# Ten kinds of VectorE stages moved behind the next score maximum in a two-layer gated attention and expert kernel

## The chip, the cores and the metric

The kernel runs on one core of a Trainium2 chip. The time is that of one launch on the device in microseconds (µs), lower is better. Three runs of the kernel before took 998.27, 994.83 and 986.67 µs; the median is 994.83.

## The reference, cut to what matters

x is 8 batches of 256 rows of 256 numbers. Two layers follow one another, each a cross attention to a context and a feed-forward part, both added to x behind a tanh gate:

```
x = x + tanh(g_xattn[0]) * attention0(layernorm(x), ctx)   # 16 heads of 16, 256 context rows
x = x + tanh(g_ffn[0])   * experts0(layernorm(x))          # sigmoid router, best 4 of 8 experts in 2 of 4 groups,
                                                           # and a shared one: (silu(x Wg) * (x Wu)) Wd
x = x + tanh(g_xattn[1]) * attention1(layernorm(x), ctx)   # the same, scores clipped to +-10000, a NaN guard
x = x + tanh(g_ffn[1])   * experts1(x)                     # softmax router, best 2 of 8: relu(x W1 + b1) W2 + b2
```

Layer 0 computes all nine experts for every row and weighs them; layer 1 sends rows only to their two experts.

## The kernel before, in words

**Slots.** Attention is cut into 16 units (layer, batch) of 8 pairs of heads. One pair is one slot, so there are 128 slots; they are counted here from 0. A slot has two halves. For each engine the kernel writes the order of its work out by hand from one table, PLAN: PLAN[2g] lists the stages of the first half of slot g, PLAN[2g+1] those of its second half. make_plan fills it: in the second halves stand, among others, the key product of a coming unit (kprod), layer statistics (stats), the division by the softmax sums (turn_values), and, alternately with the first halves, the nine gate and up products (gate_up) and nine down products (down0) of each batch in layer 0's experts, with their routing (route0, groups0, ranks0, weights0).

**TensorE in a slot** (loop over g in the tensor block): scores_by_query (L742, four matmuls into by_query), scores_by_key (L763), the stages of PLAN[2g], weigh_values (L781) in every other slot, the stages of PLAN[2g+1]. scores_by_query of a slot waits until the maximum of the slot before has been taken (max_done), because by_query is a single buffer.

**VectorE in a slot** (the loop that the diff touches): the stages of PLAN[2g-1], which are the second half of the slot before; the maximum of this slot's scores (maxima, L1354), in a unit's last slot with three small instructions behind it (shifts); the stages of PLAN[2g]; in layer 1 a clip (L1379).

**Banks.** All stages but the scores share three PSUM banks in turn (share_banks): use number i has bank i % 3, and TensorE waits before it, in open_bank, until use i - 3 has been released. For the stages of the diff VectorE is the one that releases: kprod (k_lo, L1335), turn_values (normal_done, L1391), gate_up (h_ready, L1498), down0 (x_acc, the second L1512).

**Others.** ScalarE takes the exponentials (L1152) that scores_by_key of the next slot waits for, the tanh ahead of VectorE's half of gate_up (L1185), and the normalising (L1112) behind GpSimd's square root (L1889 to L1896), which waits for VectorE's stats (L1309, L1313). The SP queue stores both parts of keys and queries and loads stacks and clip bounds. Behind the attention come the finish of layer 1's routing and 23 blocks of layer 1's experts (L998, L1014), which the change doesn't touch.

Of the kernel before, what the change touches and what calls it, by code (L numbers as in the profile page):

```python
# [100 lines left out]
def base(u):  # L101

    return LEAD + PAIRS * u
# [83 lines left out]
PLAN = make_plan()  # L187
# [1 line left out]
NORMS = [n for g in sorted(PLAN) for stage, n in PLAN[g] if stage == "stats"]  # L189
NORM_NO = {n: i for i, n in enumerate(NORMS)}  # L190
XN_NO = {n: i for i, n in enumerate(n for n in NORMS if n[0] != "finish")}
SPLITS = {}

SEMAPHORES = """ident_ready gates_in gates_ready x_in0 x_in1 x_in2 x_in3 x_in4 x_in5 x_in6 x_in7 ctx_in0 ctx_in1 attn_w_in0 attn_w_in1 wq_ready expert_in0 expert_in1 expert_in2
router_in pad_out ones_filled ctx_turned ctxT_ready ctxT_out ctxT_in0 ctxT_in1 ctxT_in2
# [49 lines left out]
def build(nc, a, out):  # L245
# [187 lines left out]
    def _(sp):  # L433
# [141 lines left out]
        def store_alternative(_):  # L575
            sp.wait_ge(sem.zalt_ready, 1)
            sp.dma_start(zalt_dram[:, :], zalt).then_inc(sem.zalt_out, 16)

        def load_alternative(_):
            sp.wait_ge(sem.zalt_out, 16)  # L580
            sp.wait_ge(sem.y_done, N0 * NB)
            sp.dma_start(alt_rows.rearrange("p b d -> p (b d)"),
                         zalt_dram.rearrange("b d -> (b d)").partition_broadcast(P)).then_inc(sem.zalt_in, 16)
# [30 lines left out]
        def first_weights(_):  # L614
            sp.wait_ge(sem.counted, NB)
            sp.dma_start(b1[:, :], a["L1_ffn_b1"]).then_inc(sem.biases_in, 16)
            sp.wait_ge(sem.block_ready, 1)
            for i in range(2):
                load_w1(i)
# [671 lines left out]
    def _(dv):  # L1291
# [57 lines left out]
        def maxima(u, p):  # L1349
            i = PAIRS * u + p  # L1350
            if p == 0 and u >= 2:
                dv.wait_ge(sem.shift_ready, 2 * (u - 1))
            dv.wait_ge(sem.qk1_done, i + 1)
            dv.tensor_reduce(rowmax[u % 2][:, :, p, :], by_query[:, :, :].rearrange("p h (t s) -> p h t s", t=TT),  # L1354
                             AX, ALU.max).then_inc(sem.max_done, 1)

        def shifts(u):
            flat = rowmax[u % 2][:, :, :, :].rearrange("p h a t -> p (h a t)")
            dv.wait_ge(sem.max_done, PAIRS * (u + 1))
            if layer_of(u):  # L1360
                dv.tensor_scalar(flat, flat, CLAMP, -CLAMP, ALU.min, ALU.max).then_inc(sem.shift_chain, 1)
                dv.wait_ge(sem.shift_chain, u + 1 + batch_of(u))
            if u:
                dv.wait_ge(sem.shift_turned, u)
            dv.tensor_scalar(shift[:, 0, :].bitcast(F32R), flat, -1.0, None, ALU.mult).then_inc(sem.shift_chain, 1)
            dv.tensor_scalar(shift[:, 2, :], flat, -1.0, -CLAMP, ALU.mult, ALU.add).then_inc(sem.shift_ready, 1)
            dv.wait_ge(sem.shift_chain, u + 1 + (batch_of(u) + 1 if layer_of(u) else 0))
            dv.scalar_tensor_tensor(shift[:, 1, :].bitcast(F32R), flat, -1.0, shift[:, 0, :], ALU.mult,
                                    ALU.subtract).then_inc(sem.shift_ready, 1)

        def clip(u, p):

            i = PAIRS * u + p
            j = i - PAIRS * NB
            prob = probs[i % 4][:, :, :, :].rearrange("p k h s -> p k (h s)")
            dv.wait_ge(lower_in[j % 3], 16 * (j // 3 + 1))
            dv.wait_ge(sem.exp_done, i + 1)
            bound = lower[j % 3][:, :, :].rearrange("p h s -> p (h s)").unsqueeze(1).broadcast_to([P, 2, 2 * S])
            dv.scalar_tensor_tensor(prob, prob, 1.0, bound, ALU.min, ALU.max).then_inc(sem.clip_done, 1)  # L1379
# [359 lines left out]
        for side in range(2):  # L1739
            op = dv.memset(stack_k[0][HALF * side + 32:HALF * side + 64, :, :].bitcast(F32), 1.0)  # L1740
        op.then_inc(sem.ones_filled, 1)
        stages = {"stats": stats, "scale_queries": scale_queries, "kprod": kprod, "qprod": qprod, "out_bias": out_bias, "bias1": bias1,
                  "turn_values": turn_values, "project": project, "route0": route0, "groups0": groups0, "ranks0": ranks0,
                  "weights0": weights0, "gate_up": gate_up, "down0": down0, "any_nan": any_nan, "spread_nan": spread_nan,
                  "mean_project": mean_project, "pick_z": pick_z, "logits1": logits1, "weights1": weights1, "sums": sums, "early_places": early_places, "blocks": blocks, "tables": tables}
        for g in range(SLOTS_IN_ALL):
            for stage, n in PLAN[2 * g - 1]:
                if stage in stages:
                    stages[stage](n)
            if g == base(0) - 2:  # L1750
                for t in values:
                    dv.memset(t[:, :, :, HD:2 * HD], 1.0)
                dv.wait_ge(sem.ident_ready, CONSTANTS)
            v, q = divmod(g - base(0), PAIRS)
            if 0 <= v < UNITS:
                maxima(v, q)
                if q == PAIRS - 1:
                    shifts(v)
            for stage, n in PLAN[2 * g]:
                if stage in stages:  # L1760
                    stages[stage](n)
            u, p = divmod(g - base(0) - LAG - 1, PAIRS)
            if NB <= u < UNITS:
                clip(u, p)
# [207 lines left out]
```

## Time and profile before

The profiled execution has a span of 991.2 µs from its first to its last instruction; its own launch time is not listed, the three runs are.

| | before |
|---|---|
| median of 3 runs | 994.83 µs (986.67 to 998.27) |
| span of the profiled execution | 991.2 µs, mean granted TensorE clock 0.941 |
| TensorE matmul busy | 902.5 µs (91%) |
| VectorE busy | 735.9 µs (74%), 1511 instructions |
| ScalarE busy | 471.3 µs (48%) |
| GpSimd busy | 243.0 µs (25%) |
| chain that ended last | TensorE 66%, VectorE 19%, issue 5%, ScalarE 3%, DMA 3%, GpSimd 2% |

The engines are called PE (TensorE matmul), PEld (its weight loads), DVE (VectorE), ACT (ScalarE) and POOL (GpSimd) in the profile. Busy time is the sum of an engine's instructions; it says nothing of which of them another engine waits for. The first maximum starts at 37.2 µs and the last at 638.2 µs; the change acts between these two.

### The profile page before, as it was taken

The page shows a single profiled execution, that of the slowest core. Times are in us where ns is not written, and L with a number is a line of the kernel's source. Part 1 is how long each engine was busy: PE and PEld are TensorE (multiplying, and loading weights), DVE is VectorE, ACT ScalarE, POOL GpSimd, SP SyncE. Part 2 cuts the span into 40 slices and gives each one's busy share as a digit, 9 for nine tenths or more (in the row PEclk, how much of TensorE's full clock was granted, in tenths as well). Part 3 has the DMA queues.
Part 4 walks back from the last instruction along what each step waited for, and adds up shares of the span by engine and source line. Part 5 has one row for each costly group of instructions (what it writes and reads, how often), then busy time and mean ns, then how long its engine had stood idle before and what let it go on. Part 6 is the DMA issues. An engine that isn't in the chain of part 4 may idle for free.

```text
span 991.2 us, 18403 instructions
## 1 busy us (share of the span) xinstructions
PE 902.5 (91%) x6561; PEld 741.6 (75%) x6561; DVE 735.9 (74%) x1511; ACT 471.3 (48%) x835; POOL 243.0 (25%) x379
## 2 busy tenths in 40 slices
PE   6788999999999998999988887888889999999995
PEld 5566777777767776777756555657779999999995
DVE  3455667777676768888896898978858888887784
ACT  2135644444534443344433444443256666666773
POOL 5010211020201000020101113323235555553332
PEclk9799999999999999999999867779799999999998
DMA  6876886055061435374554884342377766667772
GB/s 163 161 149 128 187 198 138 24 94 105 22 107 47 70 81 103 81 149 100 126 111 122 171 205 101 95 130 56 124 241 229 219 214 214 213 210 218 234 259 41
DMA packets 128524, 139.69 MB, mean 141 GB/s; under 512 B 12337, under 2 KB 121161, under 8 KB 128305
## 3 DMA queue, kind: packets, MB, share of 16 engines
q1 hardware_dynamic: 119296, 127.59, 51.7%
q0 software_dynamic: 7488, 10.39, 4.9%
q8 instruction: 53, 0.87, 0.4%
q10 hardware_dynamic: 1648, 0.53, 0.2%
q14 instruction: 39, 0.31, 0.1%
HBM read 108.50 MB, written 29.44 MB: 139 GB/s over the span
## 4 chain that ended last, share of the span: by engine, by line
PE 66%; DVE 19%; issue 5%; ACT 3%; DMA 3%; POOL 2%; SPq 1%; POOLq 0%; DVEq 0%; ACTq 0%
PE bank L1014 11%; PE bank L839 9%; PE by_query L998 7%; PE by_key L998 7%; PE bank L849 5%; DVE rowmax L1354 4%; PE value_bank L781 4%; PE by_query L742 3%; PE bank L685 3%; DVE probs L1379 3%; PE bank L808 3%; PE bank L728 2%; PE bank L694 2%; PE by_key L763 2%; DVE stats L1309 2%
## 5 line engine op out<-in xcount | busy, mean ns | idle before, releaser
L1152 ACT ACTIVATE probs<-by_key 128x1024 f32<-128x1024 f32 x128 | 130.7, 1021 | 96.8 <-PE by_key L763 96.1
L1354 DVE TENSOR_REDUCE rowmax<-by_query 128x4 f32<-128x1024 f32 x128 | 155.6, 1216 | 18.2 <-PE by_query L742 18.1
L1889 POOL TENSOR_SCALAR rstd<-moments 128x2 f32<-128x2 f32 x32 | 10.5, 328 | 504.8 <-DVE moments L1313 504.7
L1949 POOL DMA_INDIRECT out_x<-x,token_i x39 | 67.0, 1718 | 130.3 <-ACT x L1260 100.7
L742 PE MATMUL by_query<-stack_k,stack_q 48*128 48x256 f32 x512 | 68.2, 347 | 26.0 <-DVE rowmax L1354 25.5
L742 PEld LDWEIGHTS by_query<-stack_k,stack_q 48*128 48x128 f32 x512 | 41.0, 197 | 64.6 <-DVE rowmax L1354 37.3
L1014 PE MATMUL bank<-w_hi,h_hi 128*128 128x256 f32 x312 | 88.3, 283 | 0.0
L1014 PE MATMUL bank<-w_lo,h_hi 128*128 128x256 f32 x312 | 88.3, 283 | 0.0
L1014 PE MATMUL bank<-w_hi,h_lo 128*128 128x256 f32 x312 | 88.3, 283 | 0.0
L781 PE MATMUL value_bank<-probs,values 128*32 128x256 f32 x1024 | 77.3, 424 | 8.9 <-DVE probs L1379 8.7
L849 PE MATMUL bank<-w_down,hidden 128*128 128x256 f32 x288 | 80.5, 403 | 3.7 <-DVE summed L1417 1.8
L839 PE MATMUL bank<-xnT,w_gate 128*128 128x256 f32 x288 | 79.5, 400 | 3.3 <-DVE lo L1345 2.4
L1379 DVE SCALAR_TENSOR_TENSOR probs<-probs,lower 128x1024 f32<-128x1024 f32 x64 | 78.0, 1220 | 5.6 <-DMA lower<-lower 5.5
L1185 ACT ACTIVATE act_gate<-bank 128x256 f32<-128x256 f32 x72 | 27.6, 383 | 105.4 <-PE bank L839 105.4
L839 PE MATMUL bank<-xnT,w_up 128*128 128x256 f32 x288 | 75.0, 383 | 0.0
L1512 DVE SCALAR_TENSOR_TENSOR x<-bank,expert_cols,x 128x256 f32<-128x256 f32 x144 | 62.4, 476 | 15.7 <-PE bank L849 15.7
L1936 POOL DMA_INDIRECT xs_in<-rows,token_i x39 | 62.6, 1604 | 32.2 <-DVE token_i L1774 20.6
L839 PEld LDWEIGHTS bank<-xnT,w_gate 128*128 128x128 f32 x288 | 53.3, 195 | 16.1 <-DVE lo L1345 3.4
L1778 DVE TENSOR_TENSOR w_lo<-w,w_hi 128x2048 fp32r<-128x2048 f32 x23 | 52.7, 2292 | 14.8 <-ACT w_hi L1223 11.3
L849 PEld LDWEIGHTS bank<-w_down,hidden 128*128 128x128 f32 x288 | 50.7, 193 | 17.1 <-issue 3.7
L839 PEld LDWEIGHTS bank<-xnT,w_up 128*128 128x128 f32 x288 | 55.6, 193 | 7.9
L1494 DVE SCALAR_TENSOR_TENSOR act_t<-act_gate,bank 128x256 f32<-128x256 f32 x72 | 30.1, 418 | 40.7 <-ACT act_gate L1185 40.1
(263 smaller groups left out, 2237.4 us busy)
## 6 DMA issues: line engine op xcount, KB each, us to landing
w<-in_L_ffn_W SPq DMA_DIRECT2D x46, 1024.0 KB
lower<-lower SPq DMA_DIRECT2D x64, 256.0 KB, 5.4
stack_k<-qk SPq DMA_DIRECT2D x96, 128.0 KB, 5.1
stack_q<-qk SPq DMA_DIRECT2D x96, 128.0 KB, 7.0
qk<-hi SPq DMA_DIRECT2D x31, 256.0 KB, 2.4
qk<-lo SPq DMA_DIRECT2D x31, 256.0 KB, 2.7
rows<-w_gate SPq DMA_DIRECT2D x8, 264.0 KB, 4.6
x<-in_x SPq DMA_DIRECT2D x8, 256.0 KB, 7.5
```

Of the source, the lines that this page charges most:

```text
L742: mm = pe.matmul(by_query[:, side, t * S:t * S + S], sq[rows, p, t * P:t * P + P], sk[rows, p, :], start=True, stop=True)
L781: mm = pe.matmul(value_bank[32 * c:32 * c + 32, o:o + S], values[u % 2][:, kt, 4 * j + c, :], probs[(i + c // 2) % 4][:, kt, c % 2, :], st ...
L839: mm = pe.matmul(bank[:, half * S:half * S + S], w[:, k, e, :], turned_of(("ffn0", b))[:, k, :], start=k == 0, stop=k == 1)
L849: mm = pe.matmul(bank[:, t * D:t * D + D], hidden0[i % 6][:, t * P:t * P + P], w_down0[:, e, :], start=True, stop=True)
L998: mm = pe.matmul(up_bank[pair][:, half * SLOTS:half * SLOTS + SLOTS], wt[:, k, j * P:j * P + P], xt[:, k, :], start=n == 0, stop=n == len( ...
L1014: mm = pe.matmul(bank[:, t * D:t * D + D], ht[:, j, t * P:t * P + P], wt[:, j, :], start=j == 0 and t == 0 and n == 0, stop=j == JH - 1 an ...
L1152: ac.activation(probs[i % 4][:, :, :, :].rearrange("p k h s -> p h k s"), by_key[:, :, :].rearrange("p h (k s) -> p h k s", k=2), ACT.Exp) ...
L1354: dv.tensor_reduce(rowmax[u % 2][:, :, p, :], by_query[:, :, :].rearrange("p h (t s) -> p h t s", t=TT), AX, ALU.max).then_inc(sem.max_don ...
L1379: dv.scalar_tensor_tensor(prob, prob, 1.0, bound, ALU.min, ALU.max).then_inc(sem.clip_done, 1)
L1512: op = dv.scalar_tensor_tensor(xt, bank[:, t * D:t * D + D], expert_cols[b % 2][:, t, e:e + 1], xt, ALU.mult, ALU.add)
L1936: po.indirect_dma_start(xs_in[i % 4][:, t, :], None, xn1_dram[:, :], bass.IndirectOffsetOnAxis(ap=token_i[:, tiles_to(i) + t:tiles_to(i) + ...
L1949: po.indirect_dma_start(out[:, :], bass.IndirectOffsetOnAxis(ap=token_i[:, n:n + 1].bitcast(U32), axis=0), ysb[i % 3][:, t, :], None, comp ...
```

## The change

VectorE's loop takes a list of ten kinds of stages out of PLAN[2g-1] and puts them, in their old order among themselves, behind slot g's maximum (and shifts) and ahead of PLAN[2g]. Other stages of that half (project, pick_z, logits1, weights1 and so on) stay ahead of the maximum. The orders of the other engines, the banks and all instructions stay as they are.

```diff
-SPLITS = {}
+BEHIND_MAXIMA = ("down0", "stats", "turn_values", "route0", "groups0", "ranks0", "weights0", "kprod", "qprod", "gate_up")
 ...
         for g in range(SLOTS_IN_ALL):
             for stage, n in PLAN[2 * g - 1]:
-                if stage in stages:
+                if stage in stages and stage not in BEHIND_MAXIMA:
                     stages[stage](n)
 ...
                 maxima(v, q)
                 if q == PAIRS - 1:
                     shifts(v)
-            for stage, n in PLAN[2 * g]:
+            for stage, n in [(stage, n) for stage, n in PLAN[2 * g - 1] if stage in BEHIND_MAXIMA] + PLAN[2 * g]:
                 if stage in stages:
                     stages[stage](n)
```

## Rows read from the trace of the kernel before

**Rows 1.** Busy time by stretch: us, engines busy (x instructions), clock, DMA share, GB/s.
```profile
100.00:200.00 100.00, 96.50 (x679) 73.31 (x678) 70.99 (x173) 47.47 (x89) 13.19 (x41) 1.00 0.60 134
550.00:600.00 50.00, 43.26 (x291) 29.68 (x293) 40.05 (x63) 22.00 (x36) 7.92 (x18) 0.73 0.85 197
```
**Rows 2.** Waits of the whole span: who, for whom, us in total, times, longest.
```profile
DVE act_t L1494 <- ACT act_gate L1185: 40.1, 38, 3.6
...
PE by_query L742 <- DVE rowmax L1354: 25.5, 23, 3.6
...
DVE rowmax L1354 <- PE by_query L742: 18.1, 20, 2.7
...
PE value_bank L781 <- DVE probs L1379: 8.7, 10, 2.3
```
**Rows 3.** Timeline of slot 20: start, us, engine, line, idle before and its releaser.
```profile
93.86 0.50 PE L742 MATMUL by_query<-stack_k,stack_q 48*128 48x256 f32 x4
...
94.97 0.88 DVE L1335 SCALAR_TENSOR_TENSOR lo<-bank,qkb,hi 128x256 fp32r<-128x256 f32 x2 [2.93 <-ACT hi L1054]
95.77 1.22 DVE L1354 TENSOR_REDUCE rowmax<-by_query 128x4 f32<-128x1024 f32 x1
...
97.03 0.50 PE L742 MATMUL by_query<-stack_k,stack_q 48*128 48x256 f32 x4 [1.84 <-DVE rowmax L1354]
```
**Rows 4.** Timeline, scores of slot 121.
```profile
606.69 0.80 PE L742 MATMUL by_query<-stack_k,stack_q 48*128 48x256 f32 x4 [3.57 <-DVE rowmax L1354]
```
**Rows 5.** Timeline of slots 52 and 53.
```profile
246.08 0.88 DVE L1335 SCALAR_TENSOR_TENSOR lo<-bank,qkb,hi 128x256 fp32r<-128x256 f32 x2 [2.58 <-ACT hi L1054]
246.87 0.87 DVE L1512 SCALAR_TENSOR_TENSOR x<-bank,expert_cols,x 128x256 f32<-128x256 f32 x2
...
247.03 0.50 PE L742 MATMUL by_query<-stack_k,stack_q 48*128 48x256 f32 x4
...
248.19 1.03 PE L849 MATMUL bank<-w_down,hidden 128*128 128x256 f32 x4
248.21 0.42 DVE L1498 TENSOR_TENSOR hidden<-act_t,bank 128x256 f32<-128x256 f32 x1
248.55 1.22 DVE L1354 TENSOR_REDUCE rowmax<-by_query 128x4 f32<-128x1024 f32 x1
...
249.05 1.03 PE L839 MATMUL bank<-xnT,w_gate 128*128 128x256 f32 x4
...
251.25 0.84 DVE L1512 SCALAR_TENSOR_TENSOR x<-bank,expert_cols,x 128x256 f32<-128x256 f32 x2
...
253.04 1.03 PE L839 MATMUL bank<-xnT,w_gate 128*128 128x256 f32 x4
```
**Rows 6.** Timeline, the first and the last of 33 bank uses that the ledger delays.
```profile
111.38 0.42 DVE L1391 TENSOR_TENSOR attn<-bank,recip 128x256 f32<-128x256 f32 x1
...
112.75 0.95 PE L826 MATMUL bank<-gate_wT,xnT 128*128 128x8 f32 x7
...
626.38 0.42 DVE L1391 TENSOR_TENSOR attn<-bank,recip 128x256 f32<-128x256 f32 x1
...
628.19 1.12 PE L800 MATMUL bank<-ident,attn 128*128 128x128 f32 x4
```
**Rows 7.** Timeline of slots 74 and 75, the exponentials and the scores by key.
```profile
369.47 1.00 ACT L1152 ACTIVATE probs<-by_key 128x1024 f32<-128x1024 f32 x1
...
370.52 0.50 PE L763 MATMUL by_key<-stack_q,stack_k 50*128 50x256 f32 x4
```
**Rows 8.** Busy time around two waits for the maximum (columns as in rows 1), and one wait.
```profile
275.00:283.20 8.20, 6.63 (x51) 4.70 (x50) 7.71 (x24) 2.37 (x4) 0.00 (x0) 1.00 1.15 131
283.30:286.70 3.40, 3.40 (x22) 1.75 (x20) 1.76 (x4) 0.73 (x2) 0.00 (x0) 0.50 0.93 100
...
506.50:512.00 5.50, 5.50 (x41) 4.09 (x42) 5.29 (x9) 2.00 (x3) 0.00 (x0) 1.00 0.39 74
...
506.44 0.51 PE L742 MATMUL by_query<-stack_k,stack_q 48*128 48x256 f32 x4 [2.93 <-DVE rowmax L1354]
```

## The prediction

> **What bounds the kernel now.** I first read the table of busy time by stretch. Between 100 and 200 µs, and much the same up to 500, TensorE's matmuls fill nearly the whole time, with VectorE at about 70%; between 550 and 600 both are at 80 to 87% and the granted clock is only 0.73 [rows 1]. So for some 400 µs every microsecond that TensorE stands still is a microsecond of the end. Next the table of waits: the longest wait of TensorE is by_query for the maximum, 25.5 µs in 23 places, and the longest idle time of VectorE is its own wait for the tanh of gate_up, 40.1 µs [rows 2]. The waits say what could be won. They don't say what the change can lose, because that is a wait which does not exist yet; for it I read the timeline slot by slot, and asked of each moved stage who comes next for its bank and how long before that it is released today.
>
> **What moves.** 163 stages change places in slots that have a maximum: 40 down0, 32 gate_up, 28 turn_values, 25 stats, 14 kprod, and 8 each of route0, groups0 and weights0. qprod and ranks0 never stand in a second half there, so two of the ten names do nothing. No instruction is added, and none of the moved ones issues a DMA. The only queue that waits for one of them directly is SP, which stores the low part of the keys behind kprod; that part is needed seven slots later, so I cost it at nothing. If that cover were gone, each of the 14 would cost what kprod is late, up to 2.7 µs, as worked out below.
>
> **Gain: the maximum comes earlier.** Slot 20 shows it. Its scores are done at 94.36 (93.86 + 0.50), but VectorE waits for ScalarE's half of kprod, runs kprod, and starts the maximum at 95.77; the next scores wait 1.84 µs for it [rows 3]. With kprod behind it the maximum starts at 94.4, 1.36 earlier, and TensorE gets 1.36 of its 1.84 back. In each slot the gain is the smaller of two numbers: by how much the maximum can come forward, which is limited by what stays ahead of it, and how long TensorE then waits. Over all slots 20 places gain, together **13.6 µs** of the 25.5. The rest doesn't move: the longest wait, 3.57 at 606.69 [rows 4], stands behind logits1, a clip and the stats of a first half.
>
> **Loss: banks come free later.** Until now VectorE works off a second half while TensorE is still in it. Now it may not touch these stages until TensorE has finished the half, and the next scores, and the maximum has been taken. TensorE meets the banks of those stages three uses later, mostly within the same slot. Slots 52 and 53 show the price [rows 5]:
> - Before, VectorE runs kprod at 246.08, down0 at 246.87 and gate_up to 248.63 (248.21 + 0.42), and then the maximum. TensorE's uses of these banks start at 248.19 (down) and 249.05 (gate). The margin of the last is 0.42 µs.
> - After, the scores are done at 247.53, the maximum runs to 248.8, kprod to 249.7, down0 to 250.5, and gate_up, 0.9 long (248.63 − 247.74, where down0 ended), to 251.4. TensorE's gate product starts at 251.5 instead of 249.05: **2.45 late**.
> - In slot 53 the next stages wait again for the scores, now 2.45 later, and for the maximum. Taken in that slot's own time, down0, behind turn_values and one stats, ends 3.0 after its 252.09 (251.25 + 0.84); its bank's next use, at 253.04, had 0.95 to spare: another **2.06**. VectorE worked almost without a break through these slots; in the new order it stands still while TensorE finishes each half.
>
> I set up the same account for every slot: VectorE's own rows in the new order, each stage with the duration and readiness that it has in the trace, and TensorE charged with the largest lateness in the slot. 33 slots have one; the first is 0.41 (turn_values ends at 111.80, its bank's next use is at 112.75), the last 2.44 (626.80 and 628.19) [rows 6]. The sum is **38.3 µs**: 17.5 in slots 25 to 62, 18.3 in slots 65 to 104, and the last. Ten of them are above 1.5 µs.
>
> This sum has bounds. Eleven of the 33 follow a late slot directly; if the first delay gave VectorE all the time it needs, those 11.9 µs would go and 26.4 remain. The pair above, carried from the one slot into the next, keeps both, so I take the whole.
>
> **The way through ScalarE.** stats moves back too; the square root on GpSimd and the normalising follow, and behind that stands an exponential. In most places there are microseconds to spare. In slot 74 there are 0.05: the exponential ends at 370.47, the scores that wait for it start at 370.52 [rows 7]. Three such places cost 1.3 together, beyond what TensorE is late there by its banks. The clip in layer 1 stands behind the moved stages as before; VectorE's work up to it is the same, and its wait by TensorE, 8.7 µs in 10 places [rows 2], I leave as it is. It could at most about double.
>
> **Sum.** −13.6 + 38.3 + 1.3 = +26.0. The profiled execution has a span of 991.2, 3.6 below the median of the three runs; what lies around the span should not change. So the span should be about 1017, and the time 994.83 + 26 = 1021. With the bounds of the bank term alone it is +14 to +30 (the upper end with half of the clip's 8.7), 1009 to 1025: the forecast's own range.
>
> **The rivals.**
> *Worse, by clock and clip.* After 8.2 µs at 1.00 in which TensorE was busy for 6.63, the rest mostly a wait for the maximum, the granted clock falls to 0.50 (1.2 GHz) for a stretch of 3.40 µs [rows 8]. Half of it, 1.7, is lost. Against it, a wait of 2.93 before 506.44 is followed by 1.00 [rows 8], so not each wait does it. If all ten stalls above 1.5 did, it would be 17; with the clip's 8.7 the time would reach 1021 + 26 = 1047. I expect a part of that at most: 1026 to 1042.
> *It cancels.* The late stages have slack that the account doesn't see: the eleven second delays vanish and half of the rest is taken back because a stalled TensorE lets VectorE draw level. 13.2 − 13.6 leaves nothing: 995. For it speaks that VectorE is idle for a quarter of these slots; against it, that the margins in rows 5 are below 1 µs and the maximum alone takes 1.22.
> *Faster.* VectorE, not TensorE, sets the pace: the maximum fills the time in which VectorE now waits for the tanh (40.1 µs), every moved stage still ends in time, and the 13.6 are won: 981. This decides if the lateness over all slots stays below 13.6 µs, a third of the account. The slots in which VectorE works without a break, 246 to 255, speak for it; that it gets a new idle stretch ahead of the scores there speaks against it. The Trainium skill, page "Perfetto Trace Analysis", section "Optimization Strategy", advises this way: find the gaps of the engine in question, see what ends them, and make that start sooner. The trace agrees that the maximum ends the largest such gap (25.5 µs); by that rule alone the result is this rival's 981, as the page doesn't weigh what is put back for it.
>
> **Chances.** Forecast 0.57, worse 0.22, cancels 0.13, faster 0.08. About 1%, 10 µs, is what can be told from no change. The forecast and the worse case are all slower by more than that: 0.79; the cancelling case is within 1%: 0.13; faster 0.08. The range is 1000 to 1041: all of the forecast, nearly all of the worse case and the upper edge of the cancelling one, some 0.8.
>
> **What would show it.** by_query's wait for the maximum falls from 25.5 to about 12. New or longer waits of TensorE for VectorE's lines 1498, 1512, 1335 and 1391 appear at banks (gate, down, turn_values, attn_turn), together 30 µs or more. VectorE's wait for by_query rises far above its 18.1 [rows 2], and its wait for the tanh falls. The blocks of layer 1's experts keep their length. I am wrong if the bank waits stay below about 14 µs in all, or if the stretch from 100 to 500 µs, where most of them lie, doesn't become longer.

## The result

The changed kernel is slower: 1035.95 µs (1033.51 to 1039.63) against 995.05 for the kernel before, a ratio of 1.044 with a 95% interval of 1.039 to 1.049. That is +41, inside the range of 1000 to 1041, but well above the 26 of the sum, outside the forecast's own 1009 to 1025 and within the 1026 to 1042 of the worse rival. The profiled execution has a span of 1034.0 µs, 42.8 more than before. All ratios leave out runs more than 1.5% above the fastest one of their kernel; the medians and ranges take in all runs.

The busy time by stretch, as in [rows 1]: in the attention of layer 0 TensorE's matmuls fall from 96.5 to 90.6 of 100 µs and VectorE from 71.0 to 60.5. Neither engine does more; both stand still more often.

```profile
100.00:200.00 100.00, 90.58 (x591) 67.02 (x590) 60.50 (x155) 42.75 (x79) 13.07 (x39) 0.93 0.55 127
550.00:600.00 50.00, 43.17 (x293) 29.94 (x292) 40.86 (x71) 19.54 (x37) 3.13 (x8) 0.96 0.68 130
```

The table of waits of the changed kernel (who, for whom, µs, times, longest), against [rows 2]:

```profile
DVE rowmax L1354 <- PE by_query L742: 118.0, 68, 4.5
...
ACT xn L1112 <- POOL rstd L1896: 60.7, 23, 6.9
...
DVE act_t L1494 <- ACT act_gate L1185: 15.4, 19, 2.3
...
PE by_query L742 <- DVE rowmax L1354: 13.3, 14, 4.2
...
PE value_bank L781 <- DVE probs L1379: 10.3, 10, 2.3
...
PE bank L800 <- DVE attn L1391: 6.5, 7, 1.8
...
PE bank L791 <- DVE lo L1335: 5.4, 4, 1.9
...
PE bank L719 <- ACT shiftT L1141: 4.8, 1, 4.8
...
PE bank L839 <- DVE x L1512: 4.0, 4, 1.2
```

TensorE's wait for the maximum fell from 25.5 to 13.3, as forecast. VectorE's wait for the tanh fell from 40.1 to 15.4, and in its place stands a wait for the scores: 118.0 µs where there were 18.1. That is VectorE waiting to be allowed to begin with the second half. The waits for its lines 1498, 1512, 1335 and 1391 at banks, which the prediction put at 30 µs or more, are 30.6, before 4.1. Adding all rows of this table in which TensorE waits at a bank: for VectorE 15.8 µs in 18 places before, 40.0 in 45 places after; for ScalarE 15.9 before and 26.5 after (the 4.8 for shiftT in the table lie behind the last maximum). ScalarE's own wait for the square root rose from 35.7 to 60.7.

The gain at slot 20 came as worked out [rows 3]. Timeline of the changed kernel: the maximum starts as soon as the scores are there, kprod behind it, and the next scores wait 0.50 instead of 1.84.

```profile
92.91 0.50 PE L742 MATMUL by_query<-stack_k,stack_q 48*128 48x256 f32 x4
...
93.46 1.23 DVE L1354 TENSOR_REDUCE rowmax<-by_query 128x4 f32<-128x1024 f32 x1 [2.37 <-PE by_query L742]
94.60 0.87 DVE L1335 SCALAR_TENSOR_TENSOR lo<-bank,qkb,hi 128x256 fp32r<-128x256 f32 x2
...
94.74 0.50 PE L742 MATMUL by_query<-stack_k,stack_q 48*128 48x256 f32 x4 [0.50 <-DVE rowmax L1354]
```

So did the loss at slot 52 [rows 5]. VectorE stands still for 4.07 µs, takes the maximum, and works off kprod, down0 and gate_up; TensorE waits 1.87 for the first bank and a little more for the next two. Its gate product starts 4.35 after the slot's scores (267.15 − 262.80), before 2.02 (249.05 − 247.03): 2.33 late, forecast 2.45. For slot 53 the trace gives 1.90, forecast 2.06.

```profile
262.80 0.50 PE L742 MATMUL by_query<-stack_k,stack_q 48*128 48x256 f32 x4
...
263.34 1.22 DVE L1354 TENSOR_REDUCE rowmax<-by_query 128x4 f32<-128x1024 f32 x1 [4.07 <-PE by_query L742]
...
264.48 0.86 DVE L1335 SCALAR_TENSOR_TENSOR lo<-bank,qkb,hi 128x256 fp32r<-128x256 f32 x2
265.27 0.86 DVE L1512 SCALAR_TENSOR_TENSOR x<-bank,expert_cols,x 128x256 f32<-128x256 f32 x2
...
265.40 0.66 PE L791 MATMUL bank<-ident,weighted 128*128 128x128 f32 x4 [1.87 <-DVE lo L1335]
...
266.19 1.13 PE L849 MATMUL bank<-w_down,hidden 128*128 128x256 f32 x4
...
266.56 0.42 DVE L1498 TENSOR_TENSOR hidden<-act_t,bank 128x256 f32<-128x256 f32 x1
...
267.15 1.03 PE L839 MATMUL bank<-xnT,w_gate 128*128 128x256 f32 x4
```

What the forecast did not have is at slot 24, which became 3.40 µs longer (from the start of its scores to the start of the next ones) although the account gives it nothing. The stats of layer 0's first batch now stand behind the maximum and the shifts. Before, they began 3.13 ahead of the slot's scores; now they begin 0.22 behind them, 3.35 later. The square root on GpSimd ends at 108.89 (108.69 + 0.20), the normalising on ScalarE waits 3.52 for it, and behind it stand an exponential and the copy of the shifts; that copy releases the bank that TensorE needs next. First the rows of before, then those of the changed kernel:

```profile
103.27 0.75 DVE L1309 BATCH_NORM_STATS2 stats<-x 128x6 f32<-128x256 f32 x2
...
106.40 0.50 PE L742 MATMUL by_query<-stack_k,stack_q 48*128 48x256 f32 x4 [0.17 <-DVE rowmax L1354]
...
109.15 0.26 ACT L1141 ACTIVATE shiftT<-bank 64x128 f32<-64x128 f32 x1
...
109.47 0.29 PE L816 MATMUL bank<-ident,hidden 8*128 8x8 f32 x2
```

```profile
104.80 0.50 PE L742 MATMUL by_query<-stack_k,stack_q 48*128 48x256 f32 x4
...
105.02 0.75 DVE L1309 BATCH_NORM_STATS2 stats<-x 128x6 f32<-128x256 f32 x2
...
108.69 0.20 POOL L1896 TENSOR_TENSOR rstd<-rstd 128x2 f32<-128x2 f32 x1
108.98 1.09 ACT L1112 ACTIVATE xn<-x,rstd 128x256 f32<-128x256 f32 x2 [3.52 <-POOL rstd L1896]
109.98 1.00 ACT L1152 ACTIVATE probs<-by_key 128x1024 f32<-128x1024 f32 x1
110.89 0.26 ACT L1141 ACTIVATE shiftT<-bank 64x128 f32<-64x128 f32 x1
...
111.19 0.38 PE L816 MATMUL bank<-ident,hidden 8*128 8x8 f32 x2 [3.24 <-ACT shiftT L1141]
```

And the clock follows. In the 6.2 µs up to that wait's end TensorE was busy for 3.15; from 111.1 on the granted clock is 0.50 (1.2 GHz), and slots 25 and 26 are 2.06 and 1.68 longer, of which the account had 0.41. The columns are those of rows 1:

```profile
104.80:111.00 6.20, 3.15 (x21) 2.53 (x21) 2.32 (x8) 2.68 (x6) 2.13 (x8) 1.00 0.74 207
111.10:121.20 10.10, 9.84 (x54) 7.38 (x55) 4.50 (x10) 4.49 (x12) 0.00 (x0) 0.50 0.16 55
```

Slots 64 and 65 repeat the pattern with batch 4: 3.42 and 0.95 longer. There is a third place, in slot 127: the last moved stats stand behind the last maximum and its shifts, so the change acts a little beyond the last maximum, and TensorE waits 4.83 for the same copy where it waited 0.98. The first row is of before, the second of the changed kernel:

```profile
643.96 0.66 PE L719 MATMUL bank<-ident,w_gate 128*128 128x128 f32 x4 [0.98 <-ACT shiftT L1141]
...
687.12 1.11 PE L719 MATMUL bank<-ident,w_gate 128*128 128x128 f32 x4 [4.83 <-ACT shiftT L1141]
```

### The profile page after: what moved, and what is told of

Its sections match the earlier page's. It is cut to its first block, busy times and chain, and to the rows that moved or that the text cites. A ratio compares the mean times of both kernels' runs of the same rounds, so it can differ in the third digit from the quotient of the medians.

```text
span 1034.0 us, 18403 instructions
## 1 busy us (share of the span) xinstructions
PE 917.1 (89%) x6561; PEld 745.1 (72%) x6561; DVE 735.8 (71%) x1511; ACT 470.4 (45%) x835; POOL 245.7 (24%) x379
## 4 chain that ended last, share of the span: by engine, by line
PE 62%; DVE 20%; issue 8%; POOL 4%; ACT 3%; DMA 1%; SPq 1%; POOLq 0%; DVEq 0%; ACTq 0%
PE bank L1014 11%; PE bank L839 9%; PE by_query L998 7%; PE by_key L998 7%; DVE rowmax L1354 5%; PE bank L849 4%; PE by_query L742 3%; PE value_bank L781 3%; PE bank L685 3%; PE bank L728 2%; PE bank L808 2%; DVE probs L1379 2%; DVE x L1512 2%; PE bank L694 2%; DVE stats L1309 2%
## 5 line engine op out<-in xcount | busy, mean ns | idle before, releaser
L1354 DVE TENSOR_REDUCE rowmax<-by_query 128x4 f32<-128x1024 f32 x128 | 156.2, 1221 | 118.0 <-PE by_query L742 118.0
L1152 ACT ACTIVATE probs<-by_key 128x1024 f32<-128x1024 f32 x128 | 130.7, 1021 | 93.6 <-PE by_key L763 93.0
L1889 POOL TENSOR_SCALAR rstd<-moments 128x2 f32<-128x2 f32 x32 | 13.1, 409 | 548.9 <-DVE moments L1313 548.8
L781 PE MATMUL value_bank<-probs,values 128*32 128x256 f32 x1024 | 77.4, 425 | 10.4 <-DVE probs L1379 10.3
L742 PE MATMUL by_query<-stack_k,stack_q 48*128 48x256 f32 x512 | 68.4, 347 | 13.7 <-DVE rowmax L1354 13.3
L1014 PEld LDWEIGHTS bank<-w_hi,h_hi 128*128 128x128 f32 x312 | 59.9, 192 | 0.0
```

Source lines behind the costliest of these rows:

```text
L742: mm = pe.matmul(by_query[:, side, t * S:t * S + S], sq[rows, p, t * P:t * P + P], sk[rows, p, :], start=True, stop=True)
L781: mm = pe.matmul(value_bank[32 * c:32 * c + 32, o:o + S], values[u % 2][:, kt, 4 * j + c, :], probs[(i + c // 2) % 4][:, kt, c % 2, :], st ...
L1014: mm = pe.matmul(bank[:, t * D:t * D + D], ht[:, j, t * P:t * P + P], wt[:, j, :], start=j == 0 and t == 0 and n == 0, stop=j == JH - 1 an ...
L1152: ac.activation(probs[i % 4][:, :, :, :].rearrange("p k h s -> p h k s"), by_key[:, :, :].rearrange("p h (k s) -> p h k s", k=2), ACT.Exp) ...
```

## The experiments

A word on the slots: a slot's change is the distance between the starts of two successive scores, after minus before. But for e7 and e9, each experiment's edit is one function that says what goes behind the maximum; where the change asks for a name in its list, the experiments ask `behind(slot, stage, n)`. Only these functions are printed.

**e1: only where the account gives a gain.**

```diff
+GAIN_SLOTS = (4, 5, 12, 17, 20, 21, 28, 58, 77, 97, 98, 108, 109, 122)
 ...
+def behind(slot, stage, n):
+    return stage in BEHIND_MAXIMA and slot in GAIN_SLOTS
```

> All ten kinds go behind the maximum, but only in the 14 slots in which the account of the prediction gives a gain and no late bank. Theory A (a slot's effect can be read from its own rows: maximum earlier on one side, banks later on the other): 11.8 us faster than the kernel before, about 983. Theory B (the time between the maxima is set elsewhere, so that what TensorE wins in one slot it waits for in a later one): within 3 us of the kernel before. Theory C (any stage that goes behind the maximum costs): slower by 5 us or more.

Measured: 986.3 µs, ratio 0.9926 (0.9891 to 0.9961) over 12 runs: faster than the kernel before by 7 µs (4 to 11), less than 1%. Theory A's direction holds and B and C fall; the 11.8 lies just outside the interval. The largest slots show both sides: slots 12 and 20 give 1.34 each, as worked out (1.36); slots 6 and 7, behind the stats of slot 5, take 2.65 and 0.76 back. Together the 14 slots are 9.3 µs shorter in the trace, of 11.8 worked out. TensorE's wait for the maximum is 14.2 µs.

**e2: only where the account finds a late bank.**

```diff
+LATE_SLOTS = (25, 29, 32, 33, 34, 36, 40, 42, 44, 45, 52, 53, 56, 60, 61, 62, 65, 69, 72, 73, 76, 80, 82, 84, 85, 92, 93, 96, 100, 101, 102, 104, 125)
 ...
+def behind(slot, stage, n):
+    return stage in BEHIND_MAXIMA and slot in LATE_SLOTS
```

> The complement: all ten kinds go behind the maximum only in the 33 slots in which the account finds a bank that comes free late. Theory A: slower by those 38.3 us plus what the clock takes behind them, so 1033 to 1042, as slow as the change itself or slower. Theory B (the late banks are not the cause; the delays add up over all slots): the 33 slots hold about a quarter of the slots and take a share of the 41 us, some 10 to 20 us slower.

Measured: 1037.04 µs, ratio 1.043 (1.037 to 1.049). A quarter of the slots carries as much as the whole change; it also lacks the change's gain. In the trace the 33 slots are together 26.9 µs longer, of 38.3 worked out (33.7 in the changed kernel, where the clock takes more in these slots), and all other slots 9.9. TensorE's waits at banks for VectorE are 38.5 µs, nearly the changed kernel's 40.0, and those for ScalarE 14.2, no more than before. Theory A, with less in the 33 slots themselves than the account has.

**e3: the change, with two stats left ahead.**

```diff
+def behind(slot, stage, n):
+    return stage in BEHIND_MAXIMA and (stage, n) not in (("stats", ("ffn0", 0)), ("stats", ("ffn0", 4)))
```

> The change, but two of its 25 moved stats, those of batches 0 and 4 of layer 0's experts (slots 23 and 63), stay ahead of the maximum. In the changed kernel slots 24 and 64 are 3.4 us longer each, and TensorE waits there for a copy of ScalarE that stands behind the normalising. Theory A (the way through ScalarE is the cause, the bank of that copy is released late): 6.8 us faster than the changed kernel, and some 3 us more where the granted clock falls behind slot 24: 1026 to 1030. Theory B (other stages of the same slots make those waits): within 2 us of the changed kernel, 1034 to 1038.

Measured: 1022.04 µs (1016.78 to 1029.25), ratio 1.024 (1.018 to 1.030). Two stats, four small instructions each, left in their old place give back some 14 µs by the medians and 20 by the ratios, more than forecast. The trace is that of the slowest of the four runs, and its span is only 6.5 shorter than the changed kernel's. In it slots 24 to 27 are together 0.2 µs longer than before, in the changed kernel 7.1; slots 64 to 67 not at all, in the changed kernel 4.4. Other slots are longer than in the changed kernel; the clock stood at 0.50 for 89 µs between the first and the last maximum, there for 82. TensorE's wait at the gate's bank, 3.24 in the changed kernel, is gone:

```profile
107.89 1.09 ACT L1115 ACTIVATE xn<-x,rstd 128x256 f32<-128x256 f32 x2
...
109.79 0.26 ACT L1144 ACTIVATE shiftT<-bank 64x128 f32<-64x128 f32 x1
...
110.18 0.29 PE L819 MATMUL bank<-ident,hidden 8*128 8x8 f32 x2
```

**e4: the kinds that release no bank.**

```diff
+NO_BANK = ("stats", "route0", "groups0", "weights0")
 ...
+def behind(slot, stage, n):
+    return stage in NO_BANK
```

> Only stats, route0, groups0 and weights0 go behind the maximum; the four kinds whose end releases a bank stay where they were. Theory A (banks carry most of the loss): the account gives 6.8 us of gain, and the two copies of ScalarE behind the stats take as much back: within 5 us of the kernel before, 990 to 1000. Theory B (the loss comes with whatever is moved): these four kinds are 49 of the 163 stages and 56 of 153 us of VectorE's moved work, so about a third of the 41 us: 1005 to 1012.

Measured: 1025.27 µs (1017.38 to 1034.67), ratio 1.027 (1.020 to 1.034). Neither theory had that: without moving one stage that releases a bank the kernel loses some 26 µs by the ratio. In its trace, of the longest of the four runs, ScalarE waits 69.7 µs for the square root. So the way through ScalarE, which my sum had at 1.3, is a cause of its own. The next three runs take it apart.

**e5: the change without stats.**

```diff
+def behind(slot, stage, n):
+    return stage in BEHIND_MAXIMA and stage != "stats"
```

> The change without stats: the other kinds go behind the maximum, all 25 stats stay ahead of it. Theory A (banks carry the larger part, the way from stats through ScalarE adds to it): the account gives 38.3 of late banks against about 10 of gain, so +28, 1019 to 1026, some 10 to 17 us faster than the changed kernel. Theory B (the way through ScalarE is the main cause, since e4 lost 30 us without moving one stage that releases a bank): 1000 to 1010.

Measured: 1022.87 µs (1021.26 to 1024.76), ratio 1.025 (1.017 to 1.032). Theory A: the banks alone cost about what the account says. From the first to the last maximum the trace is 28.2 µs longer than before; the account without stats was 28. That the two agree so closely is in part luck: some 8 of the 28.2 are the clock's, which stood at 0.50 for 85 µs there instead of 69, and the account has no clock. TensorE waits 43.1 µs at banks for VectorE and 14.5 for ScalarE, and ScalarE 16.2 for the square root.

**e6: stats alone.**

```diff
+def behind(slot, stage, n):
+    return stage == "stats"
```

> Only the 25 stats go behind the maximum. In e4 they moved together with three routing kinds and the kernel became 30 us slower. Theory A (late stats hold up ScalarE, whose exponentials and copies TensorE needs): about as slow as e4, 1018 to 1030, with ScalarE's wait for the square root near e4's 69.7 us against 35.7 before. Theory C (the routing kinds were e4's loss): within 5 us of the kernel before, 990 to 1000.

Measured: 1029.22 µs (1017.42 to 1037.17), ratio 1.023 (1.013 to 1.034). Theory A; the routing kinds cost nothing that can be told. Its trace has slot 24 as the changed kernel has it. The rows are its waits, and two instructions of its timeline:

```profile
ACT xn L1115 <- POOL rstd L1899: 72.0, 24, 7.7
...
117.05 0.26 ACT L1144 ACTIVATE shiftT<-bank 64x128 f32<-64x128 f32 x1
...
117.36 0.32 PE L819 MATMUL bank<-ident,hidden 8*128 8x8 f32 x2 [3.23 <-ACT shiftT L1144]
```

TensorE's waits at banks for ScalarE are 26.5 µs, the same as in the changed kernel; for VectorE 22.1. With e5 that makes a cross: moving stats raises mostly the one sum, moving the others the other alone. The two ratios less one, 0.025 and 0.023, add up to 0.048; the change has 0.044.

Much of what e6 loses comes by way of the clock. In its trace TensorE stands still for 13.7 µs more than before between the first and the last maximum (61.0 and 47.3), while the clock stood at 0.50 there for 106 µs instead of 69 and behind it for 49 instead of 32; at 0.50 half of the time is lost, and half of these 54 µs is 27 of the 39.2 by which its span is longer. This is the trace of the second longest of its four runs. So that the two ratios nearly add up is no proof that the two causes simply add. The four runs, 1017, 1026, 1032 and 1037 µs, come in the order of their mean granted clock: 0.935, 0.924, 0.916, 0.914.

**e7: the change, with ScalarE's normalising put further back.**

```diff
             for stage, n in PLAN[2 * g - 1]:
-                if stage in stages:
+                if stage in stages and stage != "normal":
                     stages[stage](n)
 ...
-            for stage, n in PLAN[2 * g]:
+            for stage, n in sorted([(stage, n) for stage, n in PLAN[2 * g - 1] if stage == "normal"] + PLAN[2 * g],
+                                   key=lambda entry: entry[0] != "shift_turn"):
```

> The change, and on ScalarE the normalising of a slot's second half goes behind the slot's exponential and its copy of the shifts, which now no longer stand behind a wait for the square root. Theory A (ScalarE's order turns a late stats into a late exponential or copy): 8 to 14 us faster than the changed kernel, 1022 to 1028. Theory B (what is late is the normalised x itself, which TensorE turns in the same slot): the same or slower than the changed kernel, 1035 to 1045, with TensorE's wait for xn above its 10.5 us.

Measured: 1027.29 µs (1025.03 to 1034.67), ratio 1.030 (1.022 to 1.039): some 9 µs less than the changed kernel, within theory A, though the intervals of the two ratios meet at 1.039. The order on VectorE is that of the changed kernel; only what stands behind a late square root on ScalarE differs. ScalarE's wait for it falls to 28.0 µs. TensorE's for xn stays at 10.4, before 7.5: in slot 6 it waits 2.54 for the late normalised x itself (before 0.51), which this edit doesn't change. TensorE's waits at banks for ScalarE fall from 26.5 to 19.4, those for VectorE rise from 40.0 to 43.7.

The rise shows what the edit doesn't mend. In slot 24 the wait for the copy is gone, but now ScalarE's half of kprod stands behind the normalising, VectorE's half waits for it, and TensorE waits 2.97 for that bank; slots 24 to 27 are still 5.4 longer than before, in the changed kernel 7.1. Of the 7.8 µs by which the span of the trace is shorter than the changed kernel's, 2.9 lie in the slots and 4.7 behind the last maximum, where the clock stood at 0.50 for 27 µs instead of 39.

```profile
ACT xn L1112 <- POOL rstd L1897: 28.0, 13, 6.9
...
PE bank L719 <- ACT xn L1112: 10.4, 3, 7.0
...
112.54 0.81 ACT L1064 ACTIVATE hi<-bank,qkb 128x256 fp32r<-128x256 f32 x2
...
113.45 0.88 DVE L1346 SCALAR_TENSOR_TENSOR lo<-bank,qkb,hi 128x256 fp32r<-128x256 f32 x2 [3.73 <-ACT hi L1064]
...
114.39 0.66 PE L719 MATMUL bank<-ident,xn 128*128 128x128 f32 x4 [2.97 <-DVE lo L1346]
```

**e8: e1 without stats.**

```diff
+GAIN_SLOTS = (4, 12, 17, 20, 21, 28, 58, 77, 97, 98, 108, 109)
 ...
+def behind(slot, stage, n):
+    return stage in BEHIND_MAXIMA and stage != "stats" and slot in GAIN_SLOTS
```

> As e1, but no stats is moved (two of the 14 slots then have nothing left). In e1 the slots 6 and 7, behind the stats of slot 5, became 2.7 and 0.8 us longer. Theory A (a late stats costs through ScalarE even where its slot gains by the maximum): 2 to 3 us faster than e1, 11 to 14 us faster than the kernel before, 981 to 985. Theory B (those two slots lost time by the clock alone, and the stats moved in e1 gained elsewhere): the same as e1 or up to 2 us slower, 985 to 989.

Measured: 988.35 µs, ratio 0.9972 (0.9932 to 1.0012) over 12 runs. My theory A falls: not faster than e1, and not to be told from the kernel before. Slots 6 and 7 are indeed as long as before again (2.65 and 0.76 shorter than in e1), but others take it back: slot 21 is 1.43 longer than before (in e1 0.51), because turn_values now goes behind a stats that stays and TensorE waits 1.80 for it (in e1 0.89), and slot 22 is 1.72 longer (in e1 0.21), with the clock at 0.50 for 3.4 µs. Whether e1 is better than e8 can't be said; their intervals overlap.

**e9: the control of e7**, its edit in the kernel before. **e10:** e8 with the same edit.

> The control of e7: the kernel before, with only ScalarE's normalising behind the exponential and the copy of the shifts. Theory A (e7 won its 9 us because the stats had been made late; in the kernel before the exponentials have microseconds to spare): within 4 us of the kernel before. Theory B (the normalising ahead of the exponential costs in any order): 6 to 10 us faster, 985 to 989.

> e8 and e9 together. Theory A: as e8, within 3 us. Theory B: the sum of both, 6 to 10 us faster than e8, 973 to 978.

Measured: e9 993.47 µs, ratio 1.0013 (0.9965 to 1.0061); e10 986.54 µs, ratio 0.9958 (0.9914 to 1.0002), 12 runs each. In the kernel before the order on ScalarE makes no difference that can be told, so what e7 won goes back to the stats that had been made late. e10 is as e8. By the medians e1 and e10 are the fastest versions of this study; only e1's interval lies wholly below 1.

## Why the prediction was right, and where its sum was short

The direction and the main mechanism were right: the maximum comes earlier, the banks come free later, and the second outweighs the first. The sum was 15 µs short, and the range holds the result only because it took in the worse rival. That rival's reasons, clock and clip, explain but a part of the 15; a larger part is the way through ScalarE, and the bank term, too large, made up for some of what was missing. So that the range held is in part luck.

- **The maximum comes earlier (−13.6): right.** TensorE's wait for it fell by 12.2 µs. In e1, where only such slots change, 7 µs (4 to 11) arrive at the end.
- **Banks come free late (+38.3): right in kind, too large in size.** TensorE's waits at banks for VectorE rose by 24.2 µs. In e2, which moved only stages of the 33 slots, these are 16.3 longer in slots 25 to 62 (forecast 17.5), 9.6 in slots 65 to 104 (18.3) and 0.9 in slot 125 (2.44). At 52 and 53 the account came out: 2.33 and 1.90 (2.45 and 2.06). But seven of the 33 slots are longer by no more than 0.15 in both traces (29, 40, 56, 80, 85, 96, 104). Slot 102 is 2.81 shorter: before, the clock fell there for 3.4 µs, now it doesn't. In the changed kernel slots 32, 72 and 92 grew most, by 3.62, 3.56 and 4.00; at all three the granted clock falls to 0.50 within the slot.
- **The way through ScalarE (+1.3): the term that was mis-sized.** It is some 13 to 19 µs: the changed kernel against e5 by the medians (1035.95 and 1022.87), and by the ratios (1.044 and 1.025). I had looked at the exponentials behind the normalising and at the scores by key that wait for them [rows 7]. The expensive places are elsewhere: a copy on the same engine that releases a bank, in slots 24, 64 and 127, where a stats and the shifts of a unit meet. e3 shows it for the first two by leaving just their stats ahead. In slot 24 the stats is later by 3.35, and not only by the 1.2 of the maximum, for the shifts and the wait for the scores stand in front of it too. TensorE's waits at banks for ScalarE rose by 10.6. The spans of the changed kernel and e5 differ by 13.5, and the clock stood at 0.50 for the same 121 µs from the first maximum on in both: this term is TensorE standing still.
- **The clock and the tail: part of the worse rival, true in part.** Between the first and the last maximum the clock stood at 0.50 for 82 µs, before for 69; half of the 13 more, 7 µs, is lost. Behind the last maximum the span grew from 351.8 to 355.3 µs, and the time at 0.50 there from 32 to 39; in e6 that part took 360.1 with 49 µs at 0.50, in e7 350.6 with 27. Of the moved stages only the stats of slot 127 acts there, and both of these kernels move it; why the clock falls so differently there stays open.
- The waits add up thus: −12.2 at by_query, +24.2 and +8.8 at banks up to the last maximum, +3.5 behind it, and about +7 by the clock, 31 of the 42.8. The clip's wait rose by 1.6 and the scores by key wait 2.5 for the exponentials. Some 7 to 8 µs I can't put down to a row; most of it lies in matmuls that count as busy, for TensorE's busy time between the first and the last maximum rose from 554.9 to 567.4, 12.5, of which the clock explains 7.
- The rival "faster", with the Trainium skill's advice to find what ends the gaps of the engine in question and to make that start sooner ("Perfetto Trace Analysis", "Optimization Strategy"), is refuted for the change as a whole. In e1 the advice holds, with 7 µs gained: there it is followed only at places in which the account finds no late bank. The rival "it cancels" falls with the 41 µs; a second delay doesn't vanish behind a first, as slot 53 shows with its 1.90 behind slot 52.

## What to carry to other kernels

When a stage goes behind a wait, price it by its takers, not by its own engine: for each moved instruction find what it releases, who comes next for that, and how many nanoseconds there are between; a table of slots made from the trace before foretold the slots shown here (52 and 53) to two tenths, and over all 33 about 27 of 38 µs. Follow every chain to its end: an engine that works in order turns a late input into a lateness of all that stands behind it, here a copy that had nothing to do with the moved statistics. Putting the waiting instruction one place back moves the lateness to the next one behind it, as e7 did with kprod. An order that helps in 14 of 128 places and harms in 33 is not a rule for a kind of stage; apply it place by place.

## What the runs showed of the hardware

In the changed kernel the 6.2 µs up to the end of the wait of 3.24, in which TensorE was busy for 3.15, were followed by 10.2 µs at a granted clock of 0.50; behind the same wait in e6 it also stood there for 10.2. Of the twelve falls between the first and the last maximum of the changed kernel seven lasted 3.4. So one wait of 3.24 µs cost about 7 µs over three slots. Runs of one kernel also spread more in some kernels than in others: e6 from 1017 to 1037 µs, with mean granted clocks from 0.935 to 0.914, e5 from 1021 to 1025, with 0.932 to 0.929.
